# The delta phase's steps in another order and with other lags

## The reference, cut to what matters

```python
q, k, v = (causal_conv_silu(x @ w, conv) for w, conv in ...)   # 4 taps
q, k = l2norm(q), l2norm(k)
beta = sigmoid(x @ w_b) * 2
g = -exp(A_log) * softplus(x @ w_a + dt_bias)
# per head, over the tokens t
S = S * exp(g_t)
delta = (v_t - k_t @ S) * beta_t
S = S + outer(k_t, delta)
o_t = (q_t * scale) @ S
y = rmsnorm(o) * norm_w * silu(x @ w_g)
out = y @ w_out
```

## Time and profile before

| | |
|---|---|
| median of 3 runs | 4765.86 us (4765.37 to 4773.78) |
| span of the profiled execution | 4761.7 us (its page gives no other time for it) |
| TensorE busy | 4665.0 us, 98% |
| VectorE busy | 4138.2 us, 87% |
| ScalarE busy | 3397.1 us, 71% |
| GpSimd busy | 3152.1 us, 66% |
| delta phase | from about 87 us to about 4445 us |

### The profile page before, as it was taken

How to read it: one execution, slowest core, us unless ns; L and a number is a source line. 1 busy time by engine, 2 the same in 40 slices (tenths; PEclk the granted TensorE clock), 3 DMA queues, 4 the chain that set the end, 5 groups by cost and what they waited for, 6 DMA issues and landing times. The chain is left out here.

```text
span 4761.7 us, 140986 instructions
## 1 busy us (share of the span) xinstructions
PE 4665.0 (98%) x44336; PEld 3733.8 (78%) x44336; DVE 4138.2 (87%) x9914; ACT 3397.1 (71%) x10287; POOL 3152.1 (66%) x4511
## 2 busy tenths in 40 slices
...
DMA packets 206732, 212.94 MB, mean 45 GB/s; under 512 B 17218, under 2 KB 180180, under 8 KB 206036
## 3 DMA queue, kind: packets, MB, share of 16 engines
...
## 5 line engine op out<-in xcount | busy, mean ns | idle before, releaser
L1074 DVE SCALAR_TENSOR_TENSOR cv<-ps_a,wqkv,cv 128x511 f32<-128x511 f32 (+2 forms) x1536 | 1145.8, 746 | 181.6 <-ACT cv L1067 161.0
L1279 POOL TENSOR_TENSOR bm<-bat,mask 128x256 f16<-128x256 f32 x1536 | 1029.5, 691 | 0.6
L1059 PE MATMUL ps_a<-xin,wqkv 128*128 128x512 f32 x2048 | 1002.8, 612 | 3.0 <-DVE bat L1256 1.5
L1329 ACT ACTIVATE m<-b 128x256 f16<-128x256 f32 x1536 | 597.2, 389 | 376.2 <-PE b L1324 376.2
L1067 ACT ACTIVATE cv<-ps_a,wqkv 128x512 f32<-128x512 f32 x512 | 352.0, 688 | 554.3 <-PE ps_a L1059 554.1
L1340 DVE TENSOR_TENSOR tt<-tt,b 128x256 f16<-128x256 f16 x1536 | 635.4, 414 | 115.4 <-PE b L1335 114.8
L1382 ACT CAST tt<-bu 128x256 f16<-128x256 f32 x1536 | 578.2, 376 | 1.2 <-PE bu L1377 0.5
L1514 PE MATMUL ps_a<-wout,yT 128*128 128x256 f32 x2048 | 548.3, 390 | 0.5 <-ACT yT L1508 0.5
L1059 PEld LDWEIGHTS ps_a<-xin,wqkv 128*128 128x128 f32 x2048 | 349.6, 191 | 250.6 <-issue 250.6
L1207 PE MATMUL ps_b<-wgate,xin 128*128 128x256 f32 x2048 | 494.9, 384 | 0.2 <-DVE vtok L1230 0.2
L1256 DVE SCALAR_TENSOR_TENSOR bat<-ps_a,w,dec 128x256 f32<-128x256 f32 x1024 | 435.4, 477 | 40.5 <-DVE w L1126 22.4
...
## 6 DMA issues: line engine op xcount, KB each, us to landing
xin<-xT_scratch SPq DMA_DIRECT2D x128, 512.0 KB, 4.0
grow<-g_scratch SPq DMA_DIRECT2D x256, 256.0 KB, 4.6
gam<-g_scratch SPq DMA_DIRECT2D x256, 96.0 KB, 2.8
...
```

The lines of the kernel that those rows point to most:

```text
L1059: ins = pe.matmul(ps[:], wqkv[:, k, j * P:(j + 1) * P], xin[p][:, k, :], start=k == 0, stop=k == KT - 1)
L1074: s.done(dve.scalar_tensor_tensor(y[:, r:], ps[:, 0:T - r], tap[:, j, TAPS - 1 - r:TAPS - r], y[:, r:], ALU.mult, ALU.add), f"a_tap{j}{r}")
L1279: s.done(pool.tensor_tensor(half_of(bm[:, l, units(g), :], l, 1), half_of(bt[:, units(g), :], l, 1), half_of(c["mask"][:, l, :].unsqueeze( ...
L1329: s.done(act.mul(half_of(m1[:, l, units(g), :], l, 0), half_bank(bank, l), -1.0), f"b_Me{l}{g}")
```

## The change

`SLOT_ORDER` is another permutation of the same 269 names. Within the slot most steps have another place. The lags that change: `b_Ve01`, `b_bm11`, `b_bm21`, `b_bm31`, `b_eps`, `b_gend` and `b_kqs` go from 1 to 2; `b_lo1` and `b_Me40` from 2 to 1; `c_KS2`, `c_sq1`, `c_m1` and `c_acc0` from 3 to 2; `a_silu1` from 1 to 0. The class `Banks` works out from the list which step last used a PSUM bank; the loads' code is the same and takes the steps' semaphores as they come. The largest lags stay 3 for items and 5 for `x_` steps. The diff, with its middle and end:

```diff
 SLOT_ORDER = """
-    a_silu1.1 c_acc0.3 c_sq1.3 c_KS2.3 c_m1.3 b_Ue01.2 b_Me40.2 b_V40.2 b_M11.2 c_R2.3 b_Me11.2 b_U40.2 b_kT.1 c_p1.3
...
-    c_KS1.2 c_acc3.3 c_p0.2 b_vT1.1 b_E0 b_V20.1 a_tap02 b_U20.1 b_F1.2 b_T1.2 c_R1.2 a_proj1 k_turn.0 c_Z1.2 b_t21.1
-    b_bm01.1 b_bm11.1 b_kqs.1 c_ws.2 b_Ue20.1 b_Ve20.1 b_M30.1 b_Tq1.1 a_tap03 k_cp.0 k_prod.0 c_y0.2 a_tanh0 b_bm21.1
...
-    c_out0.2 b_bm31.1 c_S1.2 b_bm50.1 b_Ve01.1 x_x3.5 a_tanh1
+    c_R2.3 b_kT.1 b_Ve01.2 d_ln.1 b_bm11.2 k_out.1 y_turn.1 b_Ue01.2 c_p1.3 c_Z2.3 b_V40.2 c_y1.3 b_sq0.1 b_M11.2
+    c_u2.3 b_Ve40.2 b_U40.2 b_Me11.2 y_bn0 b_kk0.1 y_bn1 b_M50.2 b_bm21.2 b_V11.2 c_yT1.3 b_bm31.2 b_Ue40.2 k_mix.1
...
+    b_P0.2 d_beta.1 b_ev00.1 b_ev01.1 b_kw.1 c_S2.3 b_E1.1 d_cum.1 d_rmm.1 a_proj2.1 c_out1.3 a_cv2.1 b_Ve21.2 c_KS3.3
+    b_R0.2 b_M31.2 y_rs c_sq2.3 x_sh.5 b_gend.2 b_ktok.1 b_U21.2 c_acc1.3 b_F0.2 x_y0.5 b_bm51.2 x_y1.5 b_Ue21.2
+    b_vT0.2 c_m2.3 c_p2.3 a_proj3.1 b_hi0.1 d_cums.1 y_sh c_R3.3 b_Me31.2 c_Z3.3 b_T0.2 a_tap21.1 a_cv3.1 k_end.1
+    b_Tq0.1 c_u3.3 c_y2.3 b_vtok0.2 d_rows.1 a_tap22.1 a_tap23.1 b_V31.2 c_yT2.3 b_Ve31.2 a_tanh2.1 y_xT.1 y_xf0
+    b_g0.1 b_U31.2 b_Tf0.1 b_t20.1 b_M00.1 b_bm00.1 c_yTe2.3 b_bm10.1 a_tap31.1 a_tap32.1 a_silu2.1 b_Me00.1 b_M41.2
+    b_Me41.2 b_bm20.1 c_O3.3 b_V00.1 a_tap33.1 b_V41.2 b_Ue31.2 b_Ve00.1 b_tg0.1 b_Ve41.2 b_U41.2 b_sg0.1 c_Z0.2
+    a_tanh3.1 b_kqs.2 c_sq3.3 x_bn0.4 c_out2.3 b_M51.2 b_lo0.1 b_bm30.1 b_Ue41.2 b_M10.1 b_U00.1 b_qT.1 c_acc2.3
...
+    a_tap03 b_Me30.1 b_Tq1.1 c_yT0.2 c_Z1.2 c_yTe0.2 b_gam.1 b_t21.1 c_u1.2 b_Tf1.1 a_tap11 a_tap12 b_g1.1 c_SU1.2
...
+    c_acc0.2 b_V01.1 c_m1.2 b_U01.1
 """.split()
```

More of the change, by code:

```diff
@@ L68 @@
-    c_KS1.2 c_acc3.3 c_p0.2 b_vT1.1 b_E0 b_V20.1 a_tap02 b_U20.1 b_F1.2 b_T1.2 c_R1.2 a_proj1 k_turn.0 c_Z1.2 b_t21.1
-    b_bm01.1 b_bm11.1 b_kqs.1 c_ws.2 b_Ue20.1 b_Ve20.1 b_M30.1 b_Tq1.1 a_tap03 k_cp.0 k_prod.0 c_y0.2 a_tanh0 b_bm21.1
-    b_vtok1.1 c_yT0.2 a_cv1 b_Me30.1 a_silu0 b_Tf1.1 b_hi1.1 c_yTe0.2 b_g1.1 a_tap11 c_u1.2 a_tap12 b_V30.1 a_tap13
-    x_bn2.4 b_M01.1 b_Ve30.1 b_U30.1 b_tg1.1 c_SU1.2 b_sg1.1 x_bn3.4 c_O1.2 b_M40.1 b_Me01.1 b_V01.1 b_Ue30.1 b_U01.1
-    c_out0.2 b_bm31.1 c_S1.2 b_bm50.1 b_Ve01.1 x_x3.5 a_tanh1
+    c_R2.3 b_kT.1 b_Ve01.2 d_ln.1 b_bm11.2 k_out.1 y_turn.1 b_Ue01.2 c_p1.3 c_Z2.3 b_V40.2 c_y1.3 b_sq0.1 b_M11.2
```

9 lines of the change are left out of this document (added).

## The result

The changed kernel takes 4938.95 us in the median of 4 runs (4931.63 to 4952.04), beside it the kernel before 4766.38 us (4765.37 to 4773.78): 1.0365 times as long, 95% interval 1.0347 to 1.0383. Slower, as forecast, but by 173 us and not by 78: outside the range of 4808 to 4885.

What follows compares the result with a forecast made beforehand. TensorE, busy without a hole, was taken to bound the kernel. Terms -36 + 3 + 60 + 10 + 2 + 35 + 3 + 1 gave +78 us, a span of 4840 and a forecast of 4844 us; range 4808 to 4885.

Steps and rivals of the forecast that it cites:

- waits on TensorE from the other engines: Closest turn-rounds between TensorE and other engines in each slot: results just fit, +3 us in all, bounds 0 and 12.
- the count: TensorE's hand-overs counted in both lists: 0.28 us less per slot, an ordinary slot of 33.39 us.
- Hand-overs, -36 us: Fewer long f32 steps behind M, V or U on TensorE: 0.28 us less per slot, bounds -40 and -28.
- w_gate, +60: At 7 pair starts TensorE waits 8.6 us for w_gate, its load queued behind gam and x; bounds 56 and 74.
- w_out, +10: c_ws, now ahead of b_t21, waits for w_out's load, making b_Tq1 1.4 us late 7 times; bounds 6 and 22.
- Residual tiles, +35: In the last pair, tiles queued behind gam(i) make c_yT3 2.8 us late in 12 slots; bounds 18 and 46.
- x in every slot, +3: Each slot's x load lands with 0.9 us spare; a tenth late by 0.3 us; bounds 0 and 20.
- Fill and drain, +1: At the fill, x(2) is late once: 1 us.
- First slot of a pair, +2: b_sel gets its rows some 1.5 us late, b_Tq1 up to 0.5 us late; bounds 0 and 8.
- TensorE's order gives nothing back: Rival: reordering TensorE's steps saves nothing, the 36 us gain is absent, 4880 us; chance 0.05.

Runs made afterwards that it cites:

- lean_old: The kernel before, with TensorE no longer waiting again for a semaphore value it has already waited for: 4759.06 us, 0.9977 times before.
- new_sp: The changed kernel with only SyncE's order altered: gam(i) goes out behind x(i+1), grow(i+1) and, at pair starts, w_gate: 4824.64 us, 1.0117 times before.
- new_kqs_ss2: The changed kernel with b_kqs early in the slot, GpSimd waiting for b_ss before it, b_diag0 behind it, c_ws behind b_t21: 4851.66 us, 1.018 times before.
- best5: new_sp without TensorE's repeated waits; b_Ue31 ahead of b_Me00, c_S1 of b_Ve30; c_ws behind b_t21, x_x0 and x_x1 behind c_p3: 4744.24 us, 0.9953 times before.

## Why the prediction was wrong

- **The step that failed** is "waits on TensorE from the other engines: about nothing, +3 us", bounds 0 and 0.1 us per slot. Of the four places named there three are near waits in the trace (c_O0 behind c_yTe3, V41 behind b_Ue31, c_KS2 behind c_S1), each late by 0.1 us or less; U51 behind b_Ue00 is not, and b_Ue20 ahead of V30 I had not named. But I counted each alone, as the lateness of one result. They drain the stream, and up to three steps behind each pay for their wait instructions. Measured against the count it is 0.56 us per slot, 71 us. Shown: 0.40 of it goes with the repeated waits, 0.2 with b_Ue31 alone (the two overlap).
- **Hand-overs, -36 us**: held. From start to start (means of the ordinary slots from 1000 to 3000 us, both traces) a_proj3, b_g0, c_SU1, c_SU2, a_proj0 and c_out3 each cost 0.08 us less where they no longer stand behind M, V or U, a_proj1 0.06 less and a_proj2 0.03. c_O2 and c_Z0 behind M or U and c_O0 behind P cost 0.07 to 0.08 more, c_yT2 and b_vT1 0.03 each. The sum is -0.28 us. So the slot's +0.28 is -0.28 and +0.56, and the largest places of the second are the steps from V00 to U41 (0.22) and M21 ahead of c_O2 (0.11). a_proj1 behind c_KS1, after:

```profile
4157.06 1.88 PE L1059 MATMUL ps_a<-xin,wqkv 128*128 128x512 f32 x4
4158.78 0.28 PE L1324 MATMUL b<-tt,bm 128*128 128x64 f16 x4
```

  It costs 1.72 us from start to start, where the earlier trace rows have 1.79 for one behind a U. With the mends the new list's slot is 0.18 below the old one's 33.67, and 0.16 below lean_old's; three steps still start dry (c_O0, V30, M01). The rule of the reorder window, by which order gives nothing, has these rows against it.
- **w_gate, +60**: 59.9 us. Right in each link, and blind to what the clock does after it: 18 us more, the mis-sized part of the 87 around the pair starts.
- **w_out, +10**: the slot behind a pair's start was 35.1 to 35.4 us, 1.3 over the others, 7 times 1.3 is 9; the cause as forecast, since it stayed in new_sp and went in new_kqs_ss2 and best5, where c_ws stands behind b_t21.
- **Residual tiles, +35**: 45 measured (bounds 18 and 46): 28 in waits, most at c_yT3, and 14 by the slow clock behind them, which the sum did not have. 12 us of it stay in new_sp, where no tile is late: they are plain order.
- **x in every slot, +3**: one wait of 1.7 us; nothing. **Fill and drain, +1**: 8. **First slot of a pair, +2**: nothing is left for it in the 87 (60, 18 and 9).
- Of the 99 us between the forecast rise of 78 and the measured one of 176.7, 68 are the failed step and 32 the clock; the other differences cancel.
- The chance of 0.90 for slower was right; no rival named these waits as a cause for the ordinary slot, so the range had no room for it. The rival "TensorE's order gives nothing back" would have given a slot of 33.67, not 33.95.

"SBUF — State Buffer", section "SBUF: two separate sides", of the Trainium skill, says that VectorE and GpSimd share a port pair under an exclusive lock, taken by VectorE's faster modes or by two SBUF inputs, against a GpSimd instruction that reads SBUF. The rows of b_ss and b_w1 agree: 171 to 1754 ns and 159 to 1278 ns beside b_kqs. I had not weighed it, and my own mends fell to it twice.

"Perfetto Trace Analysis", section "Identifying Dependency Chains", of the Trainium skill, says that an instruction that waits for several engines may get separate wait instructions ahead of it. The trace agrees, with 10401 of them on TensorE's stream.
